# Another opening for an adaLN block with a state-space scan and a mixture of experts, and another order in its last stage

## The reference, cut to what matters

```python
mod = (silu(c) @ wmod).reshape(8, 6, 1, 256)        # c: 8 x 256, wmod: 256 x 1536
sa, ca, ga, sb, cb, gb = mod[:, 0], ..., mod[:, 5]  # ga, gb pushed away from 0 to at least 0.25
h = layernorm(x) * (1 + ca) + sa
x = x + ga * mamba(h)
h = layernorm(x) * (1 + cb) + sb
x = x + gb * moe(h)

# mamba(h): xn = h * rsqrt(mean(h*h) + eps) * norm_w; xi, z = split(xn @ W_in)
#   xc = silu(conv4(xi) + conv_b); dt, B, C = split(xc @ W_x); dt = softplus(dt @ W_dt + b_dt)
#   state[t] = exp(dt * A) * state[t-1] + dt * xc * B    (16 states for each of 512 channels)
#   y = sum over the states of state * C + D_skip * xc;  result h + (y * silu(z)) @ W_out
# moe(h): the top 2 of 8 experts by h @ Wg, softmax over the two; each expert
#   relu((layernorm(h) * gamma_e + beta_e) @ W1_e + b1_e) @ W2_e + b2_e + h, weighted sum
```

## Time and profile before

| | before |
|---|---|
| median of 3 runs | 1562.04 us |
| the profiled execution, its own time | 1562.95 us |
| its span, first to last instruction | 1561.1 us |
| busy in the span: PE, VectorE, ScalarE, GpSimd | 85%, 78%, 50%, 67% |
| mean granted TensorE clock | 0.923 |
| DMA | 216.61 MB, mean 139 GB/s |

### The profile page before, as it was taken

The page is one execution under the profiler, slowest core; times in us unless marked ns, Lnnn a source line. Parts: engine busy times, 40 slices in busy tenths (PEclk is TensorE's granted clock), DMA queues, the critical chain, the costliest instruction groups (busy, mean ns, idle before and its releaser), DMA issues.

```text
span 1561.1 us, 25964 instructions
## 1 busy us (share of the span) xinstructions
PE 1319.3 (85%) x7986; PEld 1072.1 (69%) x7986; DVE 1219.1 (78%) x2145; ACT 786.6 (50%) x1386; POOL 1045.2 (67%) x942
## 2 busy tenths in 40 slices
PE   3576776877877997898798799879899999999997
PEld 1244564565565765667667576768789989999997
DVE  3798999999989899989999998987355545555554
ACT  2666767867866786786787687666000000000000
POOL 2486788898989789989899988986433442221212
PEclk7887898989969899989999999989999999999999
DMA  6212121223224334244333333576967787666662
GB/s 226 69 55 84 46 54 55 95 75 88 66 85 135 113 116 131 78 144 141 100 118 99 110 113 102 182 240 209 303 165 199 203 265 216 197 193 205 190 205 78
DMA packets 129504, 216.61 MB, mean 139 GB/s; under 512 B 18236, under 2 KB 75080, under 8 KB 129240
## 3 DMA queue, kind: packets, MB, share of 16 engines
q1 hardware_dynamic: 110536, 184.12, 37.8%
q0 software_dynamic: 16064, 27.62, 7.0%
q10 hardware_dynamic: 2768, 3.21, 0.8%
HBM read 178.60 MB, written 37.22 MB: 138 GB/s over the span
## 4 chain that ended last, share of the span: by engine, by line
PE 52%; DVE 19%; issue 9%; ACT 9%; POOL 8%; DMA 1%; SPq 1%; DVEq 0%; POOLq 0%; ACTq 0%
PE psum L1680 13%; PE psum L1696 13%; DVE w_sb L1981 9%; PE psum L1491 8%; POOL dBu L877 6%; DVE y L1992 3%; PE psum L1500 3%; ACT psum L1128 3%; PE psum L1635 2%; ACT hc L1112 2%; PE psum L1457 2%; PE psum L1648 1%; DVE xc L1962 1%; DVE w_sb L1962 1%; PE psum L1480 1%
## 5 line engine op out<-in xcount | busy, mean ns | idle before, releaser
L877 POOL TENSOR_TENSOR dBu<-w_sb,brep 128x512 f32<-128x512 f32 x512 | 646.5, 1324 | 40.8 <-issue 18.1
L1981 DVE TENSOR_TENSOR_SCAN w_sb<-psum,dBu 128x512 f32<-128x512 f32 x512 | 611.4, 1211 | 58.7 <-ACT psum L1128 36.2
L1491 PE MATMUL psum<-ident,w_sb 128*128 128x128 f32 x2048 | 306.4, 297 | 124.3 <-DVE y L1992 70.5
L1128 ACT ACTIVATE psum<-w_sb,aneg 128x512 f32<-128x512 f32 x512 | 350.2, 692 | 117.2 <-DVE w_sb L1981 114.8
L1491 PEld LDWEIGHTS psum<-ident,w_sb 128*128 128x128 f32 x2048 | 250.7, 152 | 199.4 <-DVE y L1992 101.7
L864 POOL DMA_INDIRECT out<-dBu,token x59 | 92.2, 1563 | 304.5 <-DMA out<-dBu,token 204.2
L1112 ACT ACTIVATE hc<-psum,ct 128x512 f32<-128x512 f32 x256 | 175.0, 683 | 104.1 <-PE psum L1491 70.9
L1500 PE MATMUL psum<-ident,hc 128*128 128x128 f32 x1024 | 172.5, 300 | 34.4 <-ACT hc L1112 23.9
L1500 PEld LDWEIGHTS psum<-ident,hc 128*128 128x128 f32 x1024 | 134.2, 155 | 78.9 <-ACT hc L1112 37.3
L1992 DVE SCALAR_TENSOR_TENSOR y<-psum,ct,y 128x512 f32<-128x512 f32 x240 | 174.7, 728 | 12.5 <-PE psum L1491 11.8
L1680 PE MATMUL psum<-xn,win 128*128 128x128 f32 x928 | 109.9, 277 | 5.6 <-ACT xn L1215 5.6
(11 more groups left out here) (267 smaller groups left out, 1742.7 us busy)
## 6 DMA issues: line engine op xcount, KB each, us to landing
brep<-b_d SPq DMA_DIRECT2D x128, 256.0 KB
expert_pieces<-in_W SPq DMA_DIRECT2D x30, 1024.0 KB
win<-in_W SPq DMA_DIRECT2D x29, 1024.0 KB
expert_pieces<-in_W SPq DMA_DIRECT2D x42, 512.0 KB, 5.8
dBu<-rows_d SPq DMA_DIRECT2D x35, 257.0 KB
w_sb<-in_W SPq DMA_DIRECT2D x8, 1024.0 KB
xg<-rows_d SPq DMA_DIRECT2D x22, 257.0 KB, 2.8
h_d<-hmod SPq DMA_DIRECT2D x8, 512.0 KB, 3.4
```

What stands on the lines that cost most here:

```text
L877: nc.gpsimd.tensor_tensor(dBu[:, i % RING, :], u[p][:, c, :], brep[:, s % 4, :], ALU.mult).then_inc(s_dBu, 1)
L1128: nc.scalar.activation(dA[:, i % DA_RING, :], dt[p][:, c, :], ACT.Exp, scale=aneg[:, c, s:s + 1]).then_inc(s_dA, 1)
L1491: last = nc.tensor.transpose(T[:, i // DT, c * P:(c + 1) * P], hs[s % 2][:, c, i * P:(i + 1) * P], ident[:, :])
L1981: nc.vector.tensor_tensor_scan(hs[s % 2][:, c, :], dA[:, i % DA_RING, :], dBu[:, (n * UNITS + i) % RING, :], 0.0, ALU.mult, ALU.add).then_ ...
```

## The change

In the opening x of sequence 0 is loaded first, then c and the first third of the modulation weights, then the other two thirds; ScalarE issues its weight loads after the silu of c. GpSimd spreads silu(c) of sequence 0 over 128 columns (`c0`), and TensorE forms from it the first two modulation rows of sequence 0 on all partitions, in PSUM. VectorE applies them to `hmod` from there, in two halves, without the store and reload. ScalarE squares by halves and scales one of the two xnT chunks. TensorE runs 8 and 2 matmuls on zeros before and after `norm_t(0)`. xd is copied ahead of z, C's copy after the softplus, dt_proj is not interrupted by `c_t`, and VectorE does the softplus by halves. In the last stage VectorE modulates tile 13 (ahead of `o_skip`), the column load of tile 13 goes, W1 of tile 14 and then b2 are loaded after all W2 and ahead of the rows of tile 15, and in the loop the modulation of tile t+2 comes after `late_hin(t)` in place of that of tile t+1 before it.

```diff
@@ -76,7 +76,7 @@
...
 Q = psum[:, 4:6, :]
-MOD_PS = psum[:, 5:8, :]
+MOD_PS = psum[:, 1:4, :]
 YT = psum[:, 4:8, :]
@@ -198,7 +198,8 @@
...
-cts = xn[:, 0, 0:DC * NB].rearrange("p (k b) -> p k b", k=DC)
+c0 = xgT[:, :, :]
+cts = prod[:, 0:DC, :]
 wmod_sb = w2_sb[:, 6:8, :, :].rearrange("p a k d -> p (a k d)")[:, 0:DC * 6 * D].rearrange("p (k n) -> p k n", k=DC)
@@ -209,7 +210,13 @@
...
 s_w = sem("weights_loaded")
-s_ct = sem("c_loaded")
+s_ct = sem("c_and_first_modulation_loaded")
...
 s_id = sem("ident_steps")
@@ -415,9 +422,10 @@
...
 def _(sp):
+    sp.dma_start(xin[:, :, :], x[0:L, :].rearrange("(i p) d -> p i d", p=P)).then_inc(s_xin, 16)
     sp.dma_start(cts, cT.rearrange("(k p) b -> p k b", p=P)).then_inc(s_ct, 16)
-    sp.dma_start(wmod_sb, wmod.rearrange("(k p) n -> p k n", p=P)).then_inc(s_ct, 16)
-    sp.dma_start(xin[:, :, :], x[0:L, :].rearrange("(i p) d -> p i d", p=P)).then_inc(s_xin, 16)
+    sp.dma_start(wmod_sb[:, :, 0:2 * D], wmod[:, 0:2 * D].rearrange("(k p) n -> p k n", p=P)).then_inc(s_ct, 16)
+    sp.dma_start(wmod_sb[:, :, 2 * D:], wmod[:, 2 * D:].rearrange("(k p) n -> p k n", p=P)).then_inc(s_wm, 16)
     sp.dma_start(xs_of[1], x[L:2 * L, :].rearrange("(i p) d -> p i d", p=P)).then_inc(s_x1st, 16)
@@ -545,17 +553,15 @@
...
         after(sp, s_th, 2 * t - 2)
-        if t == BEGIN:
-            sp.dma_start(cols[:, t % 2, 0:FC], b1[:, bass.ds(e * FC, FC)]).then_inc(s_cl[t % 2], 16)
+        sp.dma_start(cols[:, t % 2, 0:FC], b1[:, bass.ds(e * FC, FC)]).then_inc(s_cl[t % 2], 16)
         sp.dma_start(cols[:, t % 2, FC:FC + DC], gamma[:, bass.ds(e * DC, DC)]).then_inc(s_cl[t % 2], 16)
...
     def prologue():
-        sp.dma_start(**mod_rows(0, 0, 2, modp[:, :, :])).then_inc(s_modp, 16)
+        sp.dma_start(**mod_rows(1, 0, 2, modp[:, :, :])).then_inc(s_modp, 16)
         for n in range(2, NB):
...
         store_h(0)
-        sp.dma_start(**mod_rows(1, 0, 2, modp[:, :, :])).then_inc(s_modp, 16)
         sp.wait_ge(s_modr, 2)
@@ -629,20 +635,20 @@
...
         all_w2(5)
-        sp.dma_start(b2_sb, b2.to_broadcast([P, E * D])).then_inc(s_b2, 16)
         for t in (BEGIN + 1, BEGIN + 2, BEGIN + 4):
...
         late_w1(BEGIN + 1)
-        first_columns(BEGIN + 1)
         sp.wait_ge(s_tr, NB * UNITS - TI)
...
         all_w2(7)
+        late_w1(BEGIN + 2)
+        sp.dma_start(b2_sb, b2.to_broadcast([P, E * D])).then_inc(s_b2, 16)
         late_rows(BEGIN + 3)
         for t in range(BEGIN, TILES):
-            if t + 2 < TILES:
+            if BEGIN < t and t + 2 < TILES:
                 late_w1(t + 2)
@@ -709,8 +715,8 @@
...
         h = hmod[:, :, :]
-        pool.wait_ge(s_hn, n + 1)
-        pool.wait_ge(s_modp, 16 * (n + 1))
+        pool.wait_ge(s_hn, n)
+        pool.wait_ge(s_modp, 16 * n)
         nc.gpsimd.tensor_tensor(h, h, modp[:, 1, :].unsqueeze(1).to_broadcast([P, TI, D]), ALU.mult).then_inc(pl, 1)
@@ -877,6 +883,9 @@
...
     def prologue():
+        pool.wait_ge(s_csilu, 1)
+        nc.gpsimd.tensor_tensor(c0, ones[:, :].unsqueeze(1).to_broadcast([P, DC, P]), cts[:, :, 0:1].to_broadcast([P, DC, P]),
+                                ALU.mult).then_inc(s_cb, 1)
         ln1(0, 1, 0)
@@ -984,13 +993,13 @@
...
 def _(act):
+    nc.scalar.preload_act_table_set("silu_and_others")
+    act.wait_ge(s_ct, 32)
+    nc.scalar.activation(cts, cts, ACT.Silu).then_inc(s_csilu, 1)
     for dst, src in ((win[:, :, :], W_in.rearrange("(k p) n -> p k n", p=P)),
...
         act.dma_start(dst, src).then_inc(s_w, 16)
-    nc.scalar.preload_act_table_set("silu_and_others")
-    act.wait_ge(s_ct, 32)
-    nc.scalar.activation(cts, cts, ACT.Silu).then_inc(s_csilu, 1)
@@ -1208,9 +1217,8 @@
...
         act.wait_ge(s_txp, t + 1)
-        act.wait_ge(s_cl[r], 48 * (t // 2) + (48 if t == BEGIN else 32))
-        if t == BEGIN:
-            act.wait_ge(s_thp, 2 * t)
+        act.wait_ge(s_cl[r], 48 * (t // 2 + 1))
+        act.wait_ge(s_thp, 2 * t)
         for k in range(DC):
@@ -1239,13 +1247,24 @@
...
     def prologue():
+        act.wait_ge(s_xin, 16)
+        act.wait_ge(s_ln1r, 1)
+        for i in range(TI):
+            ins = nc.scalar.activation(hmod[:, i, :], xin[:, i, :], ACT.Identity, bias=nb1[:, i:i + 1], scale=rs1[:, i:i + 1])
+            if i % 2:
+                ins.then_inc(s_hn0, 1)
         mod_copy(0)
-        act.wait_ge(s_xin, 16)
-        p_norm(0, xin, 0, lambda i: slice(i, i + 1))
+        for half in range(2):
+            act.wait_ge(s_h0, half + 1)
+            for i in (2 * half, 2 * half + 1):
+                last = nc.scalar.activation(xn[:, i, :], hmod[:, i, :], ACT.Square, scale=float(D) ** -0.5, accum_out=ssq[:, i:i + 1])
+        last.then_inc(s_sq, 1)
         mod_copy(1)
         mod_copy(2)
-        squares(0, range(TI))
         norm(0)
+        act.wait_ge(s_w, 16 * 11)
+        act.wait_ge(s_xntp, 1)
+        nc.scalar.activation(xnT[:, 1, :], Q[:, 1, :], ACT.Copy, scale=nw[:, 1:2]).then_inc(s_xnt, 1)
         act.wait_ge(s_x1st, 16)
@@ -1273,19 +1292,19 @@
...
         exps_again()
+        xd_copy(0)
         z_first(0)
         decay_rates()
-        xd_copy(0)
-        c_copy(0, 0)
         for half in range(2):
...
                 act.wait_ge(s_dtp, c + 1)
-                nc.scalar.activation(u[0][:, c, :], X0_PS[:, c, :], ACT.Abs, bias=bdt[:, c:c + 1]).then_inc(s_act, 1)
+                nc.scalar.activation(u[0][:, c, :], X0_PS[:, (c + 2) % CH, :], ACT.Abs, bias=bdt[:, c:c + 1]).then_inc(s_act, 1)
                 act.wait_ge(s_act, 2 * c + 1)
...
                                  bias=1.0).then_inc(s_sp0, 1)
+        c_copy(0, 0)
         for c in range(1, CH):
@@ -1401,7 +1420,6 @@
...
         times_c(NB - 1, 1, NS - 1, 1)
-        first_xin(BEGIN + 1)
         first_hin(BEGIN)
@@ -1420,15 +1438,20 @@
...
 def _(pe):
+    pe.wait_ge(s_ct, 32)
+    pe.wait_ge(s_cb, 1)
+    for k in range(DC):
+        last = nc.tensor.matmul(PS[:, 0, :], c0[:, k, :], wmod_sb[:, k, 0:2 * D], start=(k == 0), stop=(k == DC - 1))
+    last.then_inc(s_m0, 1)
     pe.wait_ge(s_csilu, 1)
     for j in range(3):
+        if j == 1:
+            pe.wait_ge(s_wm, 16)
         for k in range(DC):
...
     pe.wait_ge(s_id, 3)
-    pe.wait_ge(s_w, 16 * 11)
-    pe.wait_ge(s_m8, 3)
@@ -1544,11 +1567,22 @@
...
+    def warm_up(count):
+        for i in range(count):
+            nc.tensor.matmul(PS[:, 7, :], zeros[:, :], ones[:, :].unsqueeze(1).to_broadcast([P, TI, P]), start=True, stop=True)
     def prologue():
+        warm_up(8)
         norm_t(0)
-        pe.wait_ge(s_xnt, 1)
+        warm_up(2)
+        pe.wait_ge(s_w, 16 * 11)
+        pe.wait_ge(s_m8, 3)
+        pe.wait_ge(s_xn0, 1)
         for c in range(CH):
             for k in range(DC):
+                if c == 0 and k == 1:
+                    pe.wait_ge(s_xnt, 1)
                 last = nc.tensor.matmul(X0_PS[:, c, :], win[:, k, c * P:(c + 1) * P], xnT[:, k, :],
@@ -1568,11 +1602,9 @@
...
         pe.wait_ge(s_xd, 1)
-        for c in range(2):
-            nc.tensor.matmul(X0_PS[:, c, :], wdt[:, c * P:(c + 1) * P], xd[0:R, :], start=True, stop=True).then_inc(s_dtp, 1)
+        for c in range(CH):
+            nc.tensor.matmul(X0_PS[:, (c + 2) % CH, :], wdt[:, c * P:(c + 1) * P], xd[0:R, :], start=True, stop=True).then_inc(s_dtp, 1)
         c_t(0)
-        for c in range(2, CH):
-            nc.tensor.matmul(X0_PS[:, c, :], wdt[:, c * P:(c + 1) * P], xd[0:R, :], start=True, stop=True).then_inc(s_dtp, 1)
         pe.wait_ge(s_c, 1)
@@ -2067,6 +2099,15 @@
...
         x_stats(0)
+        dve.wait_ge(s_m0, 1)
+        for half in range(2):
+            dve.wait_ge(s_hn0, half + 1)
+            h = hmod[:, 2 * half:2 * half + 2, :]
+            then(nc.vector.scalar_tensor_tensor(h, PS[:, 0, D:2 * D].unsqueeze(1).to_broadcast([P, 2, D]), 1.0, h, ALU.add, ALU.mult))
+            nc.vector.tensor_tensor(h, PS[:, 0, 0:D].unsqueeze(1).to_broadcast([P, 2, D]), h, ALU.add).then_inc(s_h0, 1)
+            if half == 1:
+                dve.wait_ge(s_h0, 2)
+                nc.vector.memset(spare[:, :], 0.0).then_inc(s_h, 1)
         dve.wait_ge(s_m8, 1)
@@ -2074,18 +2115,11 @@
...
         then(nc.vector.tensor_scalar(m6[:, 4, :], m6[:, 4, :], 1.0, None, ALU.add))
-        dve.wait_ge(s_hn, 1)
-        dve.wait_ge(s_modp, 16)
-        h = hmod[:, :, :]
-        then(nc.vector.tensor_tensor(h, h, modp[:, 1, :].unsqueeze(1).to_broadcast([P, TI, D]), ALU.mult))
-        nc.vector.tensor_tensor(h, h, modp[:, 0, :].unsqueeze(1).to_broadcast([P, TI, D]), ALU.add).then_inc(s_h, 1)
         clamped(5).then_inc(s_modr, 1)
...
         dve.wait_ge(s_xntp, 1)
-        for c in range(DC):
-            last = nc.vector.tensor_scalar(xnT[:, c, :], Q[:, c, :], nw[:, c:c + 1], None, ALU.mult)
-        last.then_inc(s_xnt, 1)
+        nc.vector.tensor_scalar(xnT[:, 0, :], Q[:, 0, :], nw[:, 0:1], None, ALU.mult).then_inc(s_xn0, 1)
         for c in range(CH):
@@ -2096,11 +2130,11 @@
...
         x_stats(3)
-        for c in range(CH):
```

(14 more changed lines are left out.)

6 lines of the change are left out of this document (added).

## The result

| | before | after |
|---|---|---|
| median of 20 runs each | 1563.63 us | 1555.62 us |
| range | 1553.7 to 1567.07 | 1547.46 to 1560.26 |
| the profiled execution, its own time | 1562.95 us | 1550.88 us |
| its span | 1561.1 us | 1549.1 us |
| mean granted TensorE clock | 0.923 | 0.930 |

The ratio is 0.9944, 95% interval 0.993 to 0.9959: a gain of 8.8 us, between 6.4 and 10.9 (the two medians are 8.0 apart). One run of after, 1771.99 us at a mean granted clock of 0.72, is a slow one and left out. The forecast was 1546, a gain of 16.4, in a range that ended at 1555. The two profiled executions are 12 apart; which pieces that comes from is told with the experiments.

A forecast was written before the change was run, and what follows sets the result against it. Three pieces in a row: an opening no engine fills, scans with VectorE busy, expert tiles with TensorE busy. Terms 9.5 + 2.3 + 4.6 = 16.4 us off gave 1546 us, range 1539 to 1555.

The forecast's parts named there:

- the opening: Everything up to the first scan: 9.5 us earlier, between 6 (h lands at 32.5) and 13 (h at 28).
- the first tiles of the last stage: Tiles 13 to 15 after the scans: `first(14)` starts at 1112.3 against 1114.6, 2.3 us gained; bounds 5.0 and a loss of 3.
- order of modulation: Last stage: modulating tile t+2 earlier removes TensorE's gaps at 1156.97 (3.85) and 1206.48 (0.8); 4.6 us, bounds 3 and 6.
- Up to h: Start of the opening: x lands at 4.9, modulation weights 6.2, silu ends 6.5, halves of h ready at 12.3 and 13.8.
- The wait that takes over: Opening: `p_norm(1)` waits for the store of h, landing at 30.4; the first convolution chunk starts at 32.6, not 27.7.
- From the taps to the first scan: Opening: taps 33.4 to 42.4, x_proj ends 44.2, xd copied at 45.0; first scan 8.6 us earlier.
- at the start of the scans GpSimd sets the pace: First scans: GpSimd gets its third chunk 10.4 us earlier, so 9.5 was taken for the opening, against 8.6 at first scan.
- Rival (c): Last stage: the queue-order edit loses through rows(15), leaving 1 to 2 us in all, opening as forecast; 1551, chance 0.15.
- (b): Scans: they take back the opening's gain, only the last stage's 6.9 us stays; 1555, chance 0.12.
- (a): Opening: the store of h does not bind (lands by 28), gain 12.5 to 13 us; 1543, chance 0.2.
- (d): Last stage: slower than before, b2 and rows(15) land so late that TensorE and VectorE stand; 1567, chance 0.04.
- The last product of the opening: VectorE, opening's end: blocked in full, the second u half loses up to 1.69 instead of 0.93; gain 0.8 us less.

The follow-up runs named there:

- rows_again: The changed kernel with the rows of tile 15 issued ahead of W1 of tile 14 and b2, run a second time; 1551.11 us, ratio 0.993.
- c_early: The changed kernel, but ScalarE copies C after the first half of the softplus, not after the second; 1557.19 us, ratio 0.9952.
- rows_first: The changed kernel, but SP issues the rows of tile 15 ahead of W1 of tile 14 and b2; 1548.96 us, ratio 0.9895.
- open_only: The opening of the changed kernel with the last stage of the kernel before; 1557.33 us, ratio 0.9957 to before.
- h_first: The changed kernel, but SP stores h of sequence 0 before the modulation reload and the six x loads; 1548.17 us, ratio 0.9905.

## Why the forecast was half right

Two terms failed, the opening (9.5 forecast, 4.9 measured) and the first tiles of the last stage (2.3 forecast, -0.4 measured). In the opening three steps of the forecast were wrong: the modulation's first weights at 6.2 (7.2 to 8.1 in eleven traces of thirteen), the store of h landing at 30.4 (the normalisation that waits for it starts at 32.0 to 33.5), and the 0.9 us that were added because GpSimd was said to set the pace. In the last stage it was the rows of tile 15, forecast 24.6 us behind the last scan and used at 27.6. The other mechanisms held. By the seams, as means over the traces that share a part:

| term | forecast | measured | from |
|---|---|---|---|
| opening, to the first scan | 9.5 | 4.9 | 67.1 (four traces) less 62.2 (six) |
| first tiles of the last stage | 2.3 | -0.4 | 40.4 (four) less 40.8 (six) |
| order of modulation | 4.6 | 5.0 | 435.3 (three) less 430.3 (fourteen) |
| sum | 16.4 | 9.5 | 8.8 by the runs |

The scan stage is left out of the sum: its means differ by 2.3 (1019.9 in the four traces, 1017.6 in the six), while single traces range over 13.6.

**Up to h: right in after's trace and in rows_again, one to two us early for the eleven others** (silu at 7.2 to 8.1). In after's: x 4.66, silu 6.13, TensorE 7.19 to 10.94 (forecast 7.2 to 10.7), projection at 26.21. How x's 0.5 MB were moved stands in two windows of after (last number GB/s):

```profile
2.00:3.00 1.00, 0.00 (x0) 0.00 (x0) 0.00 (x0) 0.03 (x1) 0.85 (x8) 1.00 0.76 178
3.00:4.00 1.00, 0.00 (x0) 0.00 (x0) 0.00 (x0) 0.00 (x0) 0.20 (x1) 1.00 1.12 341
```

They hold 0.52 MB, but the first bytes of the modulation are among them: the 512 packets of x, 1 KB each, stand in the trace from 1.88 to 4.22. So x landed 0.4 after its last byte (I had 0.9). From its issue at 0.75 to its landing are 3.9 us, of which the bytes fill 2.3; 1.1 of the 1.6 that are left lie ahead of the first byte. The Trainium skill (DMA: Bandwidth & Descriptors, Anatomy of one DMA) gives about 2.0 for a transfer that GpSimd issues, most of it completion. For x, which SyncE issues, the total is somewhat lower and most of it is not completion.

**The wait that takes over: right in place, too early by 1.6.** The forecast had the store of h at 30.4; it landed at 31.98 (23.65 + 8.33). 1.2 of it is the modulation store: I had 2.2 us for its 32 KB and it took 3.20, so that the chain of the six loads began at 17.47 and not at 16.3. The other 0.4 is in the queue. Here the landing was within my bound (32.5), but the sum used the middle. In five of the six other traces with this opening and the late store it was beyond the bound: `p_norm(1)` starts at 32.9 to 33.5 (32.0 in rows_again), because the modulation came later and the reload was issued at 18.2 to 18.6. In the kernel before it was issued at 17.5 to 17.7, so in these traces the chain in front of h begins later than before, not 1.4 us earlier.

**From the taps to the first scan: late by 0.8 more.** The taps start 1.5 late (34.91 for 33.4), as the store has it. x_proj, with TensorE idle between its pairs, ends at the half clock (its last pair takes 1.80 us, its second took 1.10), and xd is copied at 47.1 where 45.0 was forecast: 2.1 late. The first scan is 2.3 late.

**A step that failed as a mechanism: "at the start of the scans GpSimd sets the pace".** My steps gave 8.6 for the first scan; I took 9.5 because GpSimd's third chunk comes 10.4 earlier. In after ScalarE's z(3) (59.81) set the first scan, and 6.3 was all that came: the product that GpSimd's third chunk waits for ends 7.8 earlier (59.63 for 67.43), and scan 64 only 6.2. c_early shows that GpSimd is close behind, as a limit and not as a gain. Where two engines meet, the later one sets the time; a gain is the smaller of the two, never the larger. So 9.5 becomes 6.3 by the store (1.6), x_proj (0.7) and this step (0.9). The 1.4 from there to the mean of 4.9 is that the trace of before stood 0.3 above its kind and the trace of after 1.2 below its own. Its early weights are part of that and not all: rows_again has them too, with its first scan at 62.4.

**First tiles: the late rows were named, and priced too low.** The forecast had the rows at 1112 for a last scan at 1087.4, 24.6 us behind it; they came at 27.6, and in five other traces with this order `late_x(15)` runs at 27.5 to 28.3. By the bytes ahead of them they should have been there; b2 took 13.5 us and not 10.6, and the rows 12.4. Rival (c) had this mechanism, the late rows, but gave the last stage 1 to 2 in all; it gave 4.6. The late rows are the 4 us that rows_first gets back. W1(13) came 0.9 later than forecast (`first(13)` 13.0 behind the last scan, not 12.1). The other half of the miss is the row that it was priced from: `first(15)` 38.8 us after the last scan in the trace of before is the best of four (38.8 to 41.9), so a term of 2.3 stood on a seam that moves by 3.

**Order of modulation: right**, both gaps gone, 5.0 for 4.6.

**Rivals.** (b), that the scans take back the opening, gave the nearest time (1555) for a wrong reason: the 6.3 us at the first scan are 6.0 at scan 256, the mean lead of the six traces over the four is 4.9 at the first scan, 4.9 at scan 64, 5.2 at scan 128 and 4.8 at scan 256, and open_only keeps its gain to the end. (a) is refuted by the 6.69 us wait. (d) didn't come: the rows cost 4, not 16. The last product of the opening took 2.17 again, 0.93 over the sum's 1.24. It starts at 57.46, beside a GpSimd product that runs from 56.23 to 58.55, so 1.09 of it overlaps. That nearly fits the rule in the Trainium skill (SBUF — State Buffer, Who interferes with whom) that the later one is blocked.

**The range** left no room for two terms that fail together: the low ends of the opening (6) and the first tiles (-3) with 4.6 sum to 7.6, 1555.3 by the profiled execution. The range had its upper end there by another path, and the median fell 0.6 beyond it. Part of that is the base: the forecast went from 1562.04, the median of 3 runs of before, and the median of 20 is 1563.63, 1.6 more. From that the same steps end the range at 1556.6. It doesn't mend the gain, which is half of what was forecast.

## What to carry to other kernels

When a step is moved earlier and the buffer it fills is overwritten later, look at the store that must read it first: its place in the DMA queue was worth as much at the first scan (4.6 us) as all the work on the opening (4.9). In a saturated queue, order by the time of need and put a wide constant last of all, also behind the small rows that the next tile wants. Price a seam from two or more traces of the same kernel: here a load at the start landed 1 to 2 us apart from run to run, and the seams moved by as much as the terms.

## What the runs showed that was not expected

- The issue itself is held up behind transfers that are under way: the six loads of x took 0.44 to 0.64 us each to issue at first, then 2.10 and 1.35 for the last two (in h_first, with the store of h ahead, 2.35 and 1.35). So h, ready at 13.8, was stored from 23.65 on: 3.2 us of that is SP's wait for the store of the modulation, 5.8 the issues. In h_first the first part is left (issue at 18.55); a kernel with the store of h ahead of that wait too was not tried.
- A scan stage of the same instructions took from 1010.6 to 1024.2 us in seventeen traces, and the same kernel gave 1023.6 and 1010.6, in executions with mean clocks of 0.929 and 0.937.
- Ten warm-up matmuls stood ahead of a projection at full clock (7.03 for 9.47 before), and leaving them out, with h stored early, cost nothing.
